# Blank rows scattered behind the tokens, expert weights fetched in thirds by ScalarE, the end of self-attention reordered, and an earlier addition on VectorE

## What is computed

```python
x = x + xattn(layernorm(x), ctx, Wq, Wk, Wv, Wo, bo)      # softmax(q k^T / 8) v, then Wo
x = x + attn(layernorm(x), wq, wk, wv, wo)                # causal, softmax, then wo
h = layernorm(x)
p = softmax(h @ router)                                   # 8 experts
w, idx = top_k(p, 2);  g = softmax(w)
x = x + sum_k g_k * (silu(h @ gate[idx_k]) * (h @ up[idx_k])) @ down[idx_k]
```

## Time and profile before

| | us |
|---|---|
| median of 3 runs (2750.82 to 2751.51) | 2751.1 |
| profiled execution, its own time | 2753.16 |
| its span (first to last instruction) | 2751.4 |
| cross-attention, to about | 1594 |
| self-attention and drain, to about | 2285 |
| experts, to the end | 2751.4 |
| PE busy, share of the span | 2217.8, 81% |
| DVE, ACT, POOL busy | 1556.3, 1300.2, 903.9 |
| mean granted TensorE clock | 0.907 |

### The profile page before, as it was taken

The page is one execution under the profiler, slowest core; times in us unless marked ns, Lnnn a source line. Parts: engine busy times, 40 slices in busy tenths (PEclk is TensorE's granted clock), DMA queues, the critical chain, the costliest instruction groups (busy, mean ns, idle before and its releaser), DMA issues. The chain is left out here.

```text
span 2751.4 us, 56741 instructions
## 1 busy us (share of the span) xinstructions
PE 2217.8 (81%) x19008; PEld 2017.0 (73%) x19008; DVE 1556.3 (57%) x3524; ACT 1300.2 (47%) x3925; POOL 903.9 (33%) x1396
## 2 busy tenths in 40 slices
PE   6998786886876776886776969999999974787796
PEld 5997775775775775775775859999999964675675
DVE  6675553553553553553553568888888863333332
ACT  5554443433443433443433447777777742333342
POOL 3332231231231231231231322455555552333333
PEclk9999987988988988988988989999999987999898
DMA  3111011011011011011010040000000012333324
GB/s 100 37 44 43 34 47 40 34 47 42 32 47 39 34 47 39 34 47 39 34 50 23 5 150 5 17 21 19 20 23 19 21 41 77 62 66 77 68 46 99
DMA packets 64363, 121.77 MB, mean 44 GB/s; under 512 B 6678, under 2 KB 46998, under 8 KB 63126
## 3 DMA queue, kind: packets, MB, share of 16 engines
q1 hardware_dynamic: 51558, 103.24, 11.1%
q0 software_dynamic: 12720, 17.47, 3.7%
HBM read 94.70 MB, written 65.05 MB: 58 GB/s over the span
## 5 line engine op out<-in xcount | busy, mean ns | idle before, releaser
L429 POOL TENSOR_TENSOR p_sb<-p_sb,rinv 128x512 f32<-128x512 f32 x256 | 279.0, 1090 | 711.3 <-DVE rinv L775 711.3
L572 PE MATMUL t_ps<-ident,p_sb 128*128 128x128 f32 x1024 | 160.3, 281 | 330.9 <-POOL p_sb L429 329.8
L572 PEld LDWEIGHTS t_ps<-ident,p_sb 128*128 128x128 f32 x1024 | 127.9, 145 | 364.4 <-POOL p_sb L429 335.7
L772 DVE COPY pt_sb<-t_ps 128x512 f32<-128x512 f32 x256 | 176.8, 690 | 358.6 <-PE t_ps L572 345.3
L47 ACT CAST qk_hi<-qk_ps 128x512 fp32r<-128x512 f32 x218 | 129.6, 594 | 452.6 <-PE qk_ps L67 443.7
L684 ACT ACTIVATE p_sb<-s_ps,nmax 128x256 f32<-128x256 f32 x512 | 238.0, 470 | 198.5 <-DVE nmax L750 194.7
L750 DVE TENSOR_REDUCE nmax<-s_ps 128x2 f32<-128x512 f32 x256 | 176.1, 688 | 206.2 <-PE s_ps L67 201.9
L1084 POOL TENSOR_TENSOR sp_sb<-sp_sb,srinv 128x512 f32<-128x512 f32 x128 | 133.1, 1040 | 230.6 <-DVE srinv L1432 228.6
L1332 ACT ACTIVATE sp_sb<-sm_sb,snmax 128x128 f32<-128x128 f32 x512 | 199.4, 390 | 5.6 <-DVE snmax L1443 2.5
L48 ACT ACTIVATE q_sb<-m_ps 64x256 fp32r<-64x256 f32 x256 | 96.8, 378 | 165.1 <-PE m_ps L67 161.3
L53 POOL TENSOR_TENSOR cx_hi<-ctx_raw,zero 128x512 fp32r<-128x512 f32 x32 | 33.2, 1039 | 428.2 <-DMA ctx_raw<-in_ctx_t 428.1
(11 more groups left out here) (339 smaller groups left out, 7793.8 us busy)
## 6 DMA issues: line engine op xcount, KB each, us to landing
xs<-blank_rows SPq DMA_DIRECT2D x13, 2517.5 KB
e_xs_in<-xs SPq DMA_DIRECT2D x69, 132.5 KB, 2.1
ctx_raw<-in_ctx_t SPq DMA_DIRECT2D x32, 256.0 KB, 3.1
ctx_raw<-in_ctx_t SPq DMA_DIRECT2D x64, 128.0 KB, 3.6
x_ring<-in_x SPq DMA_DIRECT2D x16, 256.0 KB, 2.8
x_mid<-x_ring SPq DMA_DIRECT2D x16, 256.0 KB, 48.8
e_raw<-in_gate SPq DMA_DIRECT2D x8, 512.0 KB, 3.8
e_raw<-in_up SPq DMA_DIRECT2D x8, 512.0 KB, 4.7
```

What stands on the lines that cost most here:

```text
L429: nc.gpsimd.tensor_tensor(prob, prob, inv, ALU.mult).then_inc(norm_done, 1)
L572: mm = pe.transpose(t_ps[:, k * P:(k + 1) * P], p_sb[:, (p - 3) % 4, k * P:(k + 1) * P], ident[:])
L772: nc.vector.tensor_copy(pt_sb[:, PT_SLOT[(p - 3) % PAIRS], :], t_ps[:]).then_inc(t_done, 1)
```

## The change

1. **Blank rows.** The fills of cross-attention (L383 and the one in the loop) are gone. Self-attention's SyncE now issues 8 fills of 5 tiles, one per expert, behind all its loads; GpSimd waits for them at step 7 of group 3. Every expert's region has one tile more (`CAP = NTOK + P`), and behind the last token of each expert 128 blank rows are scattered (`pad_slot`): expert 0's at the end of self-attention, the other seven at the start of GpSimd's expert block.
2. **Weights in thirds.** The next-but-one expert's weights are loaded piece by piece by ScalarE, each one a tile after the piece was split, with a semaphore per piece. Only expert 1's are still issued by SyncE. VectorE moves the next rows before it splits a piece. Expert 0's split is done in self-attention's drain, which needs `w_hi` and `w_lo` there: they become long-lived, and self-attention's weights and `xt` live in them.
3. **Drain.** The chains of small operations of `late[4]` are cut in three and put around the last addition and normalization; its 8 scatters follow behind GpSimd's last `ln_rstd`.
4. **Step 6 of self-attention.** VectorE's addition of the projection stands ahead of mask and maximum.

```diff
-        CAP = NTOK
+        CAP = NTOK + P
...
-                sp.dma_start(xs_tiles[FILLS * FILL:EXPERTS * TILES], blank_dram.unsqueeze(0).to_broadcast([FILL_REST, P, ROW])).then_inc(s_fill, DMA)
                 with sp.Fori(2, GROUPS - 1) as g:
                     load(2 * g, 0)
                     keep_x(g - 2)
                     load_x(g + 1)
                     load(2 * g + 1, 1)
-                    sp.dma_start(xs_tiles[bass.ds(FILL * g - 2 * FILL, FILL)],
-                                 blank_dram.unsqueeze(0).to_broadcast([FILL, P, ROW])).then_inc(s_fill, DMA)
...
-                load_expert(sp, 0)
+                for c in range(3):
+                    load_piece(sp, 0, c)
+                for e in range(EXPERTS):
+                    first = e * (TILES + 1)
+                    sp.dma_start(xs_tiles[first:first + MIN_TILES],
+                                 blank_dram.unsqueeze(0).to_broadcast([MIN_TILES, P, ROW])).then_inc(s_fill, DMA)
...
+                    if p == 7 and isinstance(G_, int) and G_ == 3:
+                        pool.wait_ge(s_fill, DMA * (EXPERTS + 1))
...
+                pool.wait_ge(s_late, 1)
+                dma_gate(LATE)
+                for t in range(4):
                     for k in range(2):
-                        scatter(late[4]["slot"][:, k, 2 + u:3 + u], rows[:, 2, u, :])
+                        scatter(late[4]["slot"][:, k, t:t + 1], rows[:, (LATE % 2, 2)[t // 2], t % 2, :])
...
+                pool.wait_ge(s_late, 3)
+                dma_gate(LATE + 2)
+                scatter(pad_slot[:, 0:1], blank_sb[:])
...
+                        if drain and p == 5:
+                            for c in range(3):
+                                act.wait_ge(s_raw[c], DMA)
+                                cut = slice(c * DC * F, (c + 1) * DC * F)
+                                split_hi_act(nc, w_hi[:, 0, cut], raw[:, cut]).then_inc(s_whi, 1)
...
+                second_of_two(0)
                 dve.wait_ge(ln_f["s_rstd"], GROUPS)
...
-                top_two(1)
+                both_of_two(0)
+                gates_of(0)
+                slots_late(0)
+                first_of_two(1)
+                second_of_two(1)
+                both_of_two(1)
                 gates_of(1)
                 slots_late(1)
+                dve.wait_ge(s_base, LATE + 2)
+                V.tensor_scalar(pad_slot[:], base[:], row_number[:, 0:1], None, ALU.add).then_inc(s_late, 1)
+                for c in range(3):
+                    cut = slice(c * DC * F, (c + 1) * DC * F)
+                    dve.wait_ge(s_whi, c + 1)
+                    split_lo_dve(nc, w_lo[:, 0, cut], raw[:, cut], w_hi[:, 0, cut]).then_inc(s_wlo, 1)
...
-                    if e + 2 < EXPERTS:
-                        sp.wait_ge(s_wlo, PIECES * (e + 2))
-                        load_expert(sp, e + 2)
...
+                pool.wait_ge(s_scat, (4 * GROUPS + 1) * DMA)
+                wait(pool, s_copy_gate, 0)
+                nc.gpsimd.tensor_tensor(copy_gate[:], zero[:], zero[:], ALU.add).then_inc(s_copy_gate, 1)
+                for e in range(1, EXPERTS):
+                    nc.gpsimd.indirect_dma_start(
+                        out=xs_dram, out_offset=bass.IndirectOffsetOnAxis(ap=pad_slot[:, e:e + 1], axis=0), in_=blank_sb[:],
+                        in_offset=None).then_inc(s_scat, DMA)
...
+                    kept = PIECES - 1 if e != e_before else piece - 1 if piece else None
+                    later = e + 1 if e != e_before else e + 2
+                    if kept is not None and later < EXPERTS:
+                        act.wait_ge(s_wlo, PIECES * (later - 1) + kept + 1)
+                        load_piece(nc.scalar, later, kept)
```

More of the change, by code:

```diff
@@ L1092, in group @@
                                 G.tensor_tensor(shift_f[:], zero[:].to_broadcast([P, 2]), shift_f[:], ALU.subtract).then_inc(s_shift, 1)
[L1093 to L1098, removed]
                         if not (isinstance(g, int) and g < 3):
@@ L1297, in _ @@
                 turn_final(GROUPS - 1, 3)
+                pe.wait_ge(chain, LATE_BOTH)
+                pe.wait_ge(qk_done, PAIRS * GROUPS)
+                prefix(qk_ps[1], 0, late[4]["both"], 4)
                 pe.wait_ge(sm_done, PAIRS * GROUPS - 1)
@@ L1436, in group @@
                             nc.vector.tensor_copy(pt_sb[:, p % 4, :], t_ps[:]).then_inc(t_done, 1)
+                        if p == 6 and not first:
+                            dve.wait_ge(y_mm, g)
+                            tiles = x_sb[:, bass.ds(2 * g - 2, 2), :].rearrange("p u d -> p (u d)")
+                            nc.vector.tensor_tensor(tiles, y_ps[:], tiles, ALU.add).then_inc(y_added, 1)
                         if (not first if p < LAG_S else cur):
@@ L1454, in group @@
                                          ot_hi[:, q - 1:q + 1, :].rearrange("p a t -> p (a t)")).then_inc(ot_done, 1)
-                        if p == 6 and not first:
-                            dve.wait_ge(y_mm, g)
-                            tiles = x_sb[:, bass.ds(2 * g - 2, 2), :].rearrange("p u d -> p (u d)")
-                            nc.vector.tensor_tensor(tiles, y_ps[:], tiles, ALU.add).then_inc(y_added, 1)
                         if p == 7 and not first:
@@ L1652, in moe @@
     GU = DC * F
+    xs_tiles = xs_dram.rearrange("(t p) r -> t p r", p=P)
     ROW = xs_tiles.shape[2]
+    w_hi, w_lo, s_whi, s_wlo = split
+    blank_sb, pad_slot = pads
     TAGS = EXPERTS + 1
@@ L1726, in load_tile @@
                                  xs_tiles[bass.ds(row, 1)].rearrange("t p r -> p (t r)")).then_inc(landed, DMA)
-                sp.wait_ge(s_scat, 4 * GROUPS * DMA)
-                sp.wait_ge(s_fill, DMA * (GROUPS - 1))
+                sp.wait_ge(s_scat, (4 * GROUPS + 1) * DMA)
                 load_tile(0, 0, s_xs)
@@ L1732, in _ @@
                 sp.wait_ge(s_wlo, PIECES)
-                load_expert(sp, 1)
+                for c in range(PIECES):
+                    load_piece(sp, 1, c)
                 start = 0
@@ L1737, in _ @@
                     end = sp.value_load(first_tile[0:1, e + 1:e + 2], **bound)
-                    shift = sp.value_load(region[0:1, e:e + 1], min_val=0, max_val=TILES * e) if e else 0
+                    shift = sp.value_load(region[0:1, e:e + 1], min_val=0, max_val=(TILES + 1) * e) if e else 0
+                    if e == 1:
+                        sp.wait_ge(s_scat, DMA * (4 * GROUPS + EXPERTS))
                     for i in range(0 if e else 2, MIN_TILES):
@@ L1751, in _ @@
                     load_tile(start + i, i, s_xs)
-                sp.wait_ge(s_raw, 3 * DMA * EXPERTS)
+                for c in range(PIECES):
+                    sp.wait_ge(s_raw[c], DMA * EXPERTS)
                 part = NTOK // PARTS_OUT
@@ L1884, in tile @@
                     y_copy(before, e_before)
-                act.wait_ge(s_raw, 3 * DMA)
-                for c in range(PIECES):
-                    cut = slice(c * CUT, (c + 1) * CUT)
-                    split_hi_act(nc, w_hi[:, 0, cut], raw[:, cut]).then_inc(s_whi, 1)
                 act.wait_ge(s_zero, 1)
@@ L1928, in tile @@
                     xt_lo_copy(i + 1)
+                    move(i + 2)
                     if piece is not None:
@@ L1932, in tile @@
                         split_lo_dve(nc, w_lo[:, (e + 1) % 2, cut], raw[:, cut], w_hi[:, (e + 1) % 2, cut]).then_inc(s_wlo, 1)
-                    move(i + 2)
-                for c in range(PIECES):
-                    cut = slice(c * CUT, (c + 1) * CUT)
-                    dve.wait_ge(s_whi, c + 1)
-                    split_lo_dve(nc, w_lo[:, 0, cut], raw[:, cut], w_hi[:, 0, cut]).then_inc(s_wlo, 1)
                 move(0)
```

85 lines of the change are left out of this document (41 added, 44 removed).

## The result

The changed kernel takes 2297.74 us (median of four, 2296.75 to 2298.02) against 2750.96 beside it: 0.8353 of the time, with a 95% interval of 0.8339 to 0.8368. The forecast was 2304 us, 6 above the median and within its range. The profiled execution took 2298.02, its span is 2296.3.

What follows compares the result with a forecast made beforehand. Cross-attention was bound by slow fills of 19 tiles, without them by TensorE. Gains 356.1 + 0 + 0 + 0.9 + 90 = 447.0 took the profiled 2753.2 to 2306.2, less 2.1 for the median: 2304 us, range 2292 to 2322.

Steps and rivals of the forecast that it cites:

- Cross-attention: In cross-attention from tile 2 to 30: without fills each group takes 74.46 us, gaining 356.1 us (bounds 340 to 360).
- Rival E: In cross-attention: waits and fills only coincide, stores still land late, only the experts gain; 2660 us, chance 0.01.
- rival C: In cross-attention: another wait, for rows or context, costs say 4 us a group, 56 in all; 2360 us, chance 0.05.
- Fills: In self-attention: 8 fills of 5 tiles cost 0, taking 20 us at 0.5 a tile, hidden below 141 us.
- Rival B: In self-attention: new fills run on one engine, TensorE stands still 66 us in group 3; 2370 us, chance 0.05.
- Step 6: In self-attention: TensorE's step 7 wait stays, for `sot_lo` instead of the addition; gain 0 (bounds -8 to +5.7 us).
- Drain and start: From self-attention's drain to the first silu: last scatter 1.3 us later, 2.2 saved after it; net gain 0.9 us.
- The pads: At GpSimd's start of the experts: seven scatters of blank rows take 8.8 us, hidden before the first result.
- Experts: In the 66 expert steps: of 94.5 extra us 90 are gained, 4.5 left for small collisions and first steps.
- The lower bound of 55: In the experts: smallest gain in us, if the pieces win nothing, 21 x 1.70 = 36.
- A: In the experts: ScalarE's loads still collide, delaying adds 1.5 us at 18 pieces, 27 in all; 2331 us, chance 0.14.
- D: In cross-attention: the granted clock falls, a mean of 0.73 eating the whole gain; 3494 us at half speed, chance 0.01.

Runs made afterwards that it cites:

- the 16 and 17 tiles: Kernel before the change, with fills in cross-attention's loop of 16 or 17 tiles instead of 19, the rest ahead of the loop: 2395.8 and 2620.8 us.
- the 1.5 MB at once: Changed kernel with an expert's three weight pieces loaded together directly ahead of a load of rows, by ScalarE or by SyncE: 2311.4 or 2321.8 us.
- Three at once on SyncE: Changed kernel with all three weight pieces issued in a row by SyncE, directly ahead of the load of rows of an expert's second tile: 2321.8 us.
- the pads three times: Changed kernel with the seven scatters of blank rows at GpSimd's expert start done three times, each seven after the last landed: 2316.7 us.

## Why the prediction was right

**Cross-attention**: 356.1 us worked out, 356.5 measured (1398.57 - 1042.09), with the period of the one undisturbed group that the trace of before has. Of the 359.7 up to the stage's end the other 3.2 lie ahead of tile 2 (which comes at 145.43 and 142.11). I don't credit them to the change: in the twelve kernels of the experiments tile 2 comes between 142.09 and 146.65, ten of which have the change's code up to there, so an execution's start scatters by that much. That the time of a group was the fill's, and the fill's the number of engines, is shown by the 16 and 17 tiles. Rival E (fills and waits only coincide) is out, and so is rival C (another wait takes the fill's place), with a group of 74.4 us.

**Fills**: no wait at step 7 of group 3, as said. Their time was not read rightly, though: I took 0.5 us a tile from the fill of 9, 20 us in all, and they took some 46. It made no difference below a cover of 147 us. Rival B (one engine) would have cost 60 us (66 were said).

**Step 6**: TensorE's wait is 5.4 us in 12 groups, put down to `sot_lo` (before 5.7 in 11, to the addition), as said. The groups are nonetheless 0.17 us shorter (39.69 and 39.52), 2 us in all, within the bounds; 0.07 of it is the addition's place.

**Drain and start**: from the last bias addition to the last scatter 687.26 before and 687.62 after, 0.4 later where I had 1.3; from the last scatter to the first silu 14.4 us where 14 were said. The stretch gave 1.7 us with the 2 us of self-attention in it, against 0.9. Without them little is left. To see the drain alone, take the kernel with the addition back in its old place: it has the change's drain, and its additions stand where they stood before. Its fourth-last addition and its last scatter, then the fourth-last addition of the kernel before:

```profile
1799.38 0.68 DVE L1470 TENSOR_TENSOR x_sb<-sy_ps,x_sb 128x512 f32 x1
...
1925.34 0.99 POOL L1049 DMA_INDIRECT xs<-blank_sb,pad_slot  x1 [0.16 <-issue]
```

```profile
2154.43 0.68 DVE L1458 TENSOR_TENSOR x_sb<-sy_ps,x_sb 128x512 f32 x1
```

From the addition to the last scatter are 126.0 us and were 124.2 (2278.61), so 1.8 later where 1.3 were said; to the first silu (1939.72) are 140.3 and were 140.6, so 0.3 gained where 0.9 were said. This sum of small terms can't be read from the medians: the stretch from the last bias addition to the first silu, 702.00 us, takes 701.35 to 703.85 in four kernels that have the same code there. The pads were hidden, with 8.0 us to spare (1935.3 to 1943.3).

**Experts**: 93.2 us against 90, because hardly any of the 4.5 us left for collisions occurred: nearly all steps are 5.06 to 5.08 us; the first has 6.23 and three have 5.10 to 5.34. The reading of their cause holds where it was tested: the move behind the split costs 43 us when put back, the 1.5 MB at once 13 or 22 us. The 94.5 us of the kernel before divide, by its steps, into 25.7 in the 15 steps with a piece alone, 67.5 in the six with a wait for rows, and 1.3 in others. In the six, 10 are the third piece's 1.70 (so 21 x 1.70 = 36 in all, as in the prediction), and some 57 the wait for rows and the low clock behind it. Three at once on SyncE, but with the rows moved and asked for ahead of the split, bring back only 22 of these; that the other 35 lay in the late request is what remains, but it was not measured apart. (The lower bound of 55 is by its own terms 54.)

**Rivals.** A falls by the measured length of the steps: no add delayed a copy of a result in the block, but for one wait of 6.4 us at its end. Its first premise, that ScalarE's queue protects nothing, is right; but with the weights in thirds the rows land 2.0 to 3.5 us behind their issue, and they are asked for a step of 5.07 us ahead. Its second premise, that lost time of the adds stays lost, depends on how much is lost: in the change fourteen adds come 5.2 to 5.9 us behind the one before, and others, 4.84 to 5.0 us apart, make that up (5.08 us on average, TensorE's step); a late start of 20 us was not made up. D (a low clock in a full cross-attention) falls with a clock of 1.00 over 1042 us. The forecast was 8.2 us above the profiled execution: 3.6 in cross-attention and its start, 0.8 in self-attention and drain, 3.2 in the experts, 0.5 in the tail.

## What to carry to other kernels

Where a wait names a DMA and the DMA share is near 1/16, look at the slowest dimension of the large transfer ahead of it: 16 tiles for 19 would have brought four fifths of this gain by itself. Split a big load into pieces that arrive within the time by which the small one behind them is asked ahead; another engine's queue doesn't help. A short wait on a full TensorE costs its own length and sometimes a stretch at lower clock behind it (here in 8 of 21 steps, 6 us in all). A chain of adds that wait for each other, nearly as long per step as TensorE's work, has no time to catch up a late start.

## What the runs showed that I had not expected

- A wait of 1.9 us in a nearly full TensorE can be followed by a stretch at a mean granted clock of 0.65: steps of 5.07 us became 6.77 to 8.12, not 6.77 throughout. What decides whether it comes is open; in 13 of the 21 steps, with waits of 1.70 to 1.91 us, it did not.
- Adds that each wait for the one before are close to being the next bound: in the kernel with the pads three times the first 64 adds are 5.15 us apart (1964.25 to 2288.59), in the change 5.08 (1944.25 to 2264.17), which is TensorE's step. The prediction had priced such adds at 5.01, from one pair of them.
- Three loads of 0.5 MB at once hold a load of 0.13 MB up for 1.7 us beyond its 5 us of slack when ScalarE issues them, and 2.3 us when SyncE does.
